# A pairwise-interaction tower: sums of two batches of products taken together on TensorE, with five product buffers and three weight buffers

## The chip, the cores and the metric

The kernel runs on one core of one Trainium2 chip. The metric is the device time of one execution in microseconds (us). The kernel before was run three times: 797.09, 798.48 and 800.0 us, median 798.48 us.

## The reference

For each of 2048 examples, 39 embedding rows `e` of 32 numbers are taken from 39 tables. Every pair of fields i < j gives one number through its own 32x32 matrix, and the 741 numbers, with 16 dense inputs, go through a small network:

```python
e = stack([tbl_f[ids[:, f]] for f in range(39)], axis=1)     # 2048 x 39 x 32
z = einsum('bpc,apc,bpa->bp', e[:, ROW], w, e[:, COL])         # 741 pairs
h = concatenate([z, dense_ctx], axis=1)
h = maximum(h @ W_top1 + b_top1, 0)                            # 757 -> 512
h = maximum(h @ W_top2 + b_top2, 0)                            # 512 -> 256
y = h @ W_top3                                                 # 256 -> 1
```

## The kernel before, in words

The examples are cut into NT = 4 tiles of 512 (variable `t`); examples lie along the free dimension. The 39 fields are grouped by four into 10 chunks of 128 partitions (4 fields x 32 numbers). The pairs of one tile are cut into NU = 200 units. A unit takes one field j against one chunk of up to four fields i, and so gives up to four of the 741 numbers. Units are worked in an order written out by hand (PHASES), two at a time in a step (UPS = 2) and four at a time in a batch (UPB = 4, SPB = 2 steps), so a tile has 50 batches (NBAT) and 100 steps (NS).

A unit goes through three stages.

1. `interact` (L538, matmul at L553): TensorE multiplies the unit's weights `w4` with the stacked field `e4` into PSUM `u_ps`. `u_ps` has room for two steps: step s waits until step s-2 has been multiplied (L541).
2. `multiply` (L844, instruction at L851): VectorE multiplies the two units of a step, straight from `u_ps`, with the embeddings `eT` into a product buffer `prod`. There are PR = 4 product buffers of one step each. Step s waits for its matmuls (L846) and until step s-PR has been summed (L848).
3. `reduce` (L564, matmul at L577): TensorE sums each product over 32 partitions with a 0/1 matrix `sel`, into one of the four 32-partition quadrants of PSUM `z_ps`. A batch has four such matmuls, each of them two matmul records in the trace. Units in different quadrants run at the same time; the quadrant of each unit is fixed by PLACES. Six `z_ps` tiles fill per tile of examples; ScalarE copies each to `zT` when its last unit is summed (`take_z`, L721 and L784 to L789).

The order on TensorE is written out (L639 to L656). For batch b: the two steps of `interact`; a piece of the top network of the tile before (`mlp_piece`, L590 to L594, two records each; none in the first tile, and 34 or 36 of the 50 batches have one otherwise); `reduce` of batch b-1; a `turn` (transposes of gathered rows into `t_ps`, L513), if one is due; and table look-ups (`look_up`, L532), if any are due. A look-up finds rows of the small tables by multiplying bf16 parts of the table with 0/1 matrices `one_hot`, which VectorE makes (L839) one batch ahead. Look-ups, too, write 32-partition quadrants. In the last tile, batches 40 to 49 also begin the top network for that tile itself (`early_piece`, L604), and `finish` (L606) completes it.

The order on VectorE (L881 to L893) for batch b: the two multiplies, then `split_chunk` if a chunk is complete, then the `one_hot` of batch b+1.

SyncE issues the loads in an order of its own (L479 to L493). Weights come as 25 pieces per tile (8 units, two batches each) into a ring `w4` of WR = 4 places. At every second batch the piece that stands WR-1 = 3 pieces ahead is loaded (`bring_piece`, L402), after the steps of batch b-1 have been issued (`s_u`, L410). On the same queue stand the stores of `parts` and the loads of `e4`. GpSimd gathers rows of the big tables, paced by the count of multiplies (L388).

Of the kernel before, what the change touches and what calls it, by code (L numbers as in the profile page):

```python
# [81 lines left out]
UPB = 4  # L82
NBAT = NU // UPB
# [28 lines left out]
ER = 4  # L112
PW = 8
NPW = NU // PW
WR = 4
ES = 4

PACED_FROM, PACE_LEAD = 96, 40

E4_SLOT = {0: 0, 1: 2, 2: 3, 3: 1, 7: 2, 8: 3, 4: 0, 5: 1, 6: 0, 9: 1}  # L120
OS = 3
PR = 4

TWO_PLACES = (0, 1, 2, 3, 7)

# [110 lines left out]
def mlp_pieces(batch, last):  # L236
    return [piece for piece, b in zip(MLP, MLP_AT[last]) if b == batch]


def ends_tile(tile):  # L240
    return max(u for u in range(NU) if PLACES[u][0] == tile)
# [10 lines left out]
def tower(nc, tables, ids, hot_ids, hot_rows, dense, w, w1, b1, w2, b2, w3, sel_in, ident_in, y):  # L252
# [4 lines left out]
    with ExitStack() as ctx:  # L257
        def sb(name, shape, dt=F32):
            return ctx.enter_context(nc.sbuf_tensor(name, shape, dt))

        def sem(name):
            return ctx.enter_context(nc.semaphore(name))

        w4 = sb("w4", [P, WR, PW * P], F32R)
        eT = sb("eT", [P, NG + len(TWO_PLACES), NB])
        e_rows = sb("e_rows", [P, ER, TPG, P])
        parts = sb("parts", [P, 2, 2, NB], F32R)
        e4 = sb("e4", [P, ES, C, NB], F32R)
        prod = sb("prod", [P, PR, UPS, NB])
        zT = sb("zT", [P, 2, NZ, NB])  # L270
# [72 lines left out]
        s_wout = [sem(f"s_wout{r}") for r in range(2)]  # L343
        s_w4 = [sem(f"s_w4{r}") for r in range(WR)]
        s_rows = [sem(f"s_rows{r}") for r in range(ER)]
# [19 lines left out]
        def e_slot(t, g):  # L365
            return NG + TWO_PLACES.index(g) if t % 2 and g in TWO_PLACES else g
# [34 lines left out]
        def _(sp):  # L401
            def bring_piece(t, p):  # L402
                n = NPW * t + p
                if n >= NPW * NT:
                    return
                if t == 0:
                    prep = [k for k, (a, b) in enumerate(PREP_UNITS) if a <= PW * p < b][0]
                    sp.wait_ge(s_wout[prep % 2], 64 * (prep // 2 + 1))
                if n >= WR:
                    sp.wait_ge(s_u, (n - WR + 1) * PW // UPS)  # L410
                sp.dma_start(w4[:, n % WR, :].bitcast(F32), w_rows.rearrange("a h x n -> (a h x) n")[:, PW * P * p:PW * P * (p + 1)]
                             ).then_inc(s_w4[n % WR], 16)

# [19 lines left out]
            def store_parts(c):  # L433
                t, g = c
                n = POS[c]
                rows = D * fields_in(g)
                here = scratch[t, g, 0:fields_in(g)].rearrange("j a h n -> (j a) h n")
                sp.wait_ge(s_eh, n + 1)
                sp.dma_start(here[:, 0, :], parts[0:rows, n % 2, 0, :].bitcast(F32)).then_inc(s_scr[n % 2], 16)
                sp.wait_ge(s_el, n + 1)  # L440
                sp.dma_start(here[:, 1, :], parts[0:rows, n % 2, 1, :].bitcast(F32)).then_inc(s_scr[n % 2], 16)
# [30 lines left out]
            stack_chunk((0, 0))  # L472
            stack_chunk((0, 1))
            store_parts((0, 2))
            bring_piece(0, 2)
            stack_chunk((0, 2))
            sp.dma_start(dense_g[:, :, :, :], dense.rearrange("t p n d -> p t (n d)").rearrange("p t (n d) -> p t n d", d=DENSE)).then_inc(s_dense, 16)

# [17 lines left out]
        def _(pe):  # L496
# [67 lines left out]
            def reduce(t, batch):  # L564
                pe.wait_ge(s_mul, NS * t + SPB * (batch + 1))
                if batch == NBAT - 1:
                    add_dense(t)
                for n in range(SPB * batch, SPB * (batch + 1)):
                    slots = [e_slot(t, UNITS[UPS * n + i][1]) for i in range(UPS)]
                    for i in range(UPS):  # L570
                        u = UPS * n + i
                        tile, quad, row = PLACES[u]
                        z = NZ * t + tile
                        if u in OPENS_TILE and z >= 2:
                            pe.wait_ge(s_zc, z - 1)
                        place = i if slots[0] <= slots[1] else 1 - i
                        last = nc.tensor.matmul(z_ps[D * quad:D * quad + D, z % 2, :],  # L577
                                                sel[:, D - 1 - row:2 * D - 1 - row], prod[:, (NS * t + n) % PR, place, :],
                                                start=u in OPENS, stop=u in CLOSES, skip_group_check=True)
                    last.then_inc(s_red, 1)  # L580
# [25 lines left out]
            def finish(t):  # L606
                pe.wait_ge(s_mul, NS * (t + 1))
                for m in (2, 3):
                    for k in range(NZ - 1):
                        if k == NZ - 2:  # L610
                            pe.wait_ge(s_zc, NZ * t + NZ - 1)
                        nc.tensor.matmul(end_ps[m], w1s[:, k, m * P:m * P + P], zT[:, t % 2, k, :], start=k == 0, stop=False)  # L612
                reduce(t, NBAT - 1)
                pe.wait_ge(s_zc, NZ * (t + 1))
                for m in range(H1 // P):
                    nc.tensor.matmul(end_ps[m], w1s[:, NZ - 1, m * P:m * P + P], zT[:, t % 2, NZ - 1, :],
                                     start=False, stop=True).then_inc(s_m, 1)
                for k in range(H1 // P):
                    pe.wait_ge(s_mc, NI * t + k + 1)
                    for m in range(H2 // P):  # L620
                        last = nc.tensor.matmul(end_ps[ITEM[2, m]], w2s[:, k, m * P:m * P + P], h1[:, k, :],  # L621
                                                start=k == 0, stop=k == H1 // P - 1)
                        if k == H1 // P - 1:
                            last.then_inc(s_m, 1)
                for k in range(H2 // P):
                    pe.wait_ge(s_mc, NI * t + ITEM[2, k] + 1)
                    last = nc.tensor.matmul(end_ps[ITEM[3, 0]][0:1, :], w3s[:, k:k + 1], h2[:, t % 2, k, :],
                                            start=k == 0, stop=k == H2 // P - 1)
                last.then_inc(s_m, 1)
# [9 lines left out]
            for t in range(NT):  # L639
                for b in range(NBAT):  # L640
                    for x in range(SPB):
                        interact(t, SPB * b + x)
                    if t:
                        for piece in mlp_pieces(b, t == NT - 1):
                            mlp_piece(t - 1, *piece)
                    if b:
                        reduce(t, b - 1)
                    elif t:
                        reduce(t - 1, NBAT - 1)
                    for c in TURNS.get(NBAT * t + b, ()):  # L650
                        turn(c)
                    for c, k in TAKES.get(NBAT * t + b, ()):
                        look_up(c, k)
                    if t == NT - 1:
                        for m, k in EARLY.get(b, ()):
                            early_piece(t, m, k)  # L656
            finish(NT - 1)

        @block.scalar
        def _(act):  # L660
# [109 lines left out]
            for t in range(NT):  # L770
                for b in range(NBAT):
                    if t == 0 and b in PREPS:
                        weights_high(PREPS[b])
                        weights_rest(PREPS[b])
                    if t == 0 and b in PREP_LOADS:
                        load_weights(PREP_LOADS[b])
                    if t == 0 and b == LAST_TABLE_BATCH:
                        table_high(HOT_CHUNKS[-1])
                        table_middle(HOT_CHUNKS[-1])
                    if t:  # L780
                        for layer, m, k in mlp_pieces(b, t == NT - 1):
                            if k == LAYER_INPUTS[layer] - 1:
                                take_mlp(t - 1, layer, m, m_ps[:, :])
                    for tile in range(NZ):  # L784
                        done = ends_tile(tile) // UPB + 1
                        if done == b:
                            take_z(t, tile)
                        elif t and done == NBAT and b == 0:
                            take_z(t - 1, tile)  # L789
                    for c in COMPLETE.get(NBAT * t + b, ()):  # L790
                        take_chunk(c)
            t = NT - 1
# [6 lines left out]
        def _(dve):  # L799
# [44 lines left out]
            def multiply(t, n):  # L844
                s = NS * t + n
                dve.wait_ge(s_u, s + 1)  # L846
                if s >= PR:
                    dve.wait_ge(s_red, s - PR + 1)  # L848
                a, b = sorted(e_slot(t, UNITS[UPS * n + i][1]) for i in range(UPS))
                e = eT[:, a:b + 1:b - a, :] if a != b else eT[:, a:a + 1, :].broadcast_to([P, UPS, NB])  # L850
                nc.vector.tensor_tensor(prod[:, s % PR, :, :], u_ps[:, s % 2, :, :], e, ALU.mult).then_inc(s_mul, 1)  # L851

# [100 lines left out]
```

## Time and profile before

| | us |
|---|---|
| median of three runs | 798.48 |
| the profiled execution | 801.8 |
| its span, first to last instruction | 799.6 |
| TensorE matmuls busy | 725.3 (91%) |
| VectorE busy | 635.5 (79%) |
| GpSimd busy | 422.2 (53%) |
| ScalarE busy | 94.2 (12%) |

Busy time is the time in which an engine has an instruction in work. The ends of matmuls are modelled and matmuls overlap, so the start of one group to the start of the next says more than a duration. The mean granted TensorE clock was 0.966 of full speed; the stretches with less lie in the first 170 us and for a moment near 239 us.

### The profile page before, as it was taken

The numbers are of one execution on the slowest core, as the hardware profiler recorded it, in microseconds if no ns is written. First come the engines' busy times: TensorE is split into PE (matmuls) and PEld (weight loads), VectorE is DVE, ScalarE is ACT, GpSimd is POOL, SyncE is SP. The second block draws the span as 40 slices with busy tenths as digits, with TensorE's granted clock in tenths as the row PEclk, the third lists the DMA queues.
The fourth block names the chain that finished last, engine by engine and source line by source line (L and its number), as shares of the span: only waits on it lengthen the run. The fifth ranks groups of instructions, "written<-read, shape, count | busy, mean of one in ns | idle before, by whom it ended". The sixth has DMA issues, their size and how long they took to land.

```text
span 799.6 us, 11291 instructions
## 1 busy us (share of the span) xinstructions
PE 725.3 (91%) x4378; PEld 289.6 (36%) x4378; DVE 635.5 (79%) x792; ACT 94.2 (12%) x170; POOL 422.2 (53%) x463
## 2 busy tenths in 40 slices
PE   1647387899989999999999999999999999999998
PEld 0212132333323344444333344444333444443343
DVE  3738679899987999889987898879969887778650
ACT  3211101011101000101111010110111010011002
POOL 6899999931565555555556555555655565100000
PEclk9777789999999999999999999999999999999999
DMA  7694838668878638264765655446765445443300
GB/s 212 227 321 168 280 96 276 224 198 302 287 254 300 246 90 261 66 220 160 249 207 169 220 133 197 134 146 227 232 221 158 157 153 195 163 137 94 118 0 1
DMA packets 75713, 149.88 MB, mean 187 GB/s; under 512 B 13621, under 2 KB 22920, under 8 KB 75532
## 3 DMA queue, kind: packets, MB, share of 16 engines
q1 hardware_dynamic: 52772, 125.30, 45.4%
q10 hardware_dynamic: 10600, 17.55, 6.4%
q0 software_dynamic: 12288, 6.32, 5.2%
q8 instruction: 35, 0.57, 0.3%
q14 instruction: 18, 0.15, 0.1%
HBM read 115.49 MB, written 33.62 MB: 186 GB/s over the span
## 4 chain that ended last, share of the span: by engine, by line
PE 73%; DVE 13%; DMA 6%; issue 5%; ACT 2%; ACTq 1%; SPq 0%; DVEq 0%
PE z_ps L577 23%; PE u_ps L553 22%; PE t_ps L532 10%; PE m_ps L590 8%; DVE prod L851 7%; DVE one_hot L839 4%; PE m_ps L592 3%; DMA e<-scratch 3%; PE t_ps L513 2%; DMA w_rows<-h 1%; PE u_ps L612 1%; ACTq L710 1%; PE u_ps L621 1%; DMA h<-in_w_dram 1%; PE m_ps L594 1%
## 5 line engine op out<-in xcount | busy, mean ns | idle before, releaser
L851 DVE TENSOR_TENSOR prod<-u_ps,eT 128x1024 f32<-128x1024 f32 x400 | 469.8, 1217 | 100.5 <-PE u_ps L553 100.1
L389 POOL DMA_INDIRECT e_rows<-in_tbl_dram,idx x384 | 379.1, 987 | 263.3 <-DVE prod L851 190.1
L553 PE MATMUL u_ps<-e,w 128*128 128x512 f32 x800 | 256.3, 434 | 45.0 <-DMA e<-scratch 21.6
L577 PE MATMUL z_ps<-prod,sel 128*32 128x512 f32 x1600 | 264.1, 614 | 0.0
L553 PEld LDWEIGHTS u_ps<-e,w 128*128 128x128 f32 x800 | 133.7, 190 | 184.8 <-DVE prod L851 86.7
L532 PE MATMUL t_ps<-one_hot,tb 125*32 125x512 bf16 x1560 | 158.6, 405 | 11.3 <-DVE one_hot L839 11.2
L839 DVE TENSOR_SCALAR one_hot<-hot_idx,row 125x512 bf16<-125x512 f16 (+2 forms) x320 | 136.3, 479 | 9.8 <-PE t_ps L532 7.7
L532 PEld LDWEIGHTS t_ps<-one_hot,tb 125*32 125x32 bf16 x1560 | 57.7, 101 | 109.5 <-issue 76.6
L577 PEld LDWEIGHTS z_ps<-prod,sel 128*32 128x32 f32 x1600 | 43.9, 108 | 139.4 <-issue 112.7
L590 PE MATMUL m_ps<-zT,w1s 128*128 128x512 f32 x144 | 73.5, 592 | 0.0
L671 ACT CAST parts<-t_ps 128x512 fp32r<-128x512 f32 (+1 forms) x40 | 23.5, 587 | 263.3 <-PE t_ps L532 158.7
L397 POOL MEMSET w1s<- 128x512 f32 x75 | 43.1, 574 | 0.0
L724 ACT COPY zT<-z_ps 128x512 f32<-128x512 f32 x24 | 14.1, 588 | 206.0 <-PE z_ps L577 206.0
L805 DVE TENSOR_TENSOR parts<-eT,parts 128x512 fp32r<-128x512 f32 (+1 forms) x40 | 27.2, 680 | 3.4 <-ACT eT L676 3.4
L590 PEld LDWEIGHTS m_ps<-zT,w1s 128*128 128x128 f32 x144 | 27.1, 188 | 6.3
L513 PE MATMUL t_ps<-ident,e_rows 128*128 128x128 f32 (+2 forms) x112 | 19.0, 294 | 6.4 <-ACT eT L676 6.4
L592 PE MATMUL m_ps<-h,w2s 128*128 128x512 f32 x48 | 24.5, 592 | 0.0
L676 ACT COPY eT<-t_ps 128x512 f32<-128x512 f32 (+1 forms) x40 | 23.6, 591 | 0.0
L513 PEld LDWEIGHTS t_ps<-ident,e_rows 128*128 128x128 f32 (+2 forms) x112 | 11.6, 136 | 29.9 <-issue 28.8
L731 ACT ACTIVATE h<-m_ps,b1s 128x512 f32<-128x512 f32 x13 | 9.0, 689 | 111.9 <-PE m_ps L590 110.7
L812 DVE TENSOR_TENSOR h<-h 128x512 fp32r<-128x512 f32 (+1 forms) x13 | 8.6, 662 | 10.7 <-ACT h L689 10.7
L689 ACT CAST h<-h 128x512 fp32r<-128x512 f32 (+1 forms) x13 | 7.9, 608 | 43.0 <-DMA w_rows<-h 30.1
(42 smaller groups left out, 101.1 us busy)
## 6 DMA issues: line engine op xcount, KB each, us to landing
w<-w_rows SPq DMA_DIRECT2D x100, 512.0 KB, 6.2
e<-scratch SPq DMA_DIRECT2D x72, 512.0 KB, 4.6
scratch<-parts SPq DMA_DIRECT2D x72, 256.0 KB
w_rows<-h ACTq DMA_DIRECT2D x48, 256.0 KB
e_rows<-in_tbl_dram,idx POOLq DMA_INDIRECT x384
hot_idx<-hot SPq DMA_DIRECT2D x12, 512.0 KB, 5.8
h<-in_w_dram ACTq DMA_DIRECT2D x12, 256.0 KB, 3.3
e<-scratch SPq DMA_DIRECT2D x8, 384.0 KB
```

Of the source, the lines that this page charges most:

```text
L389: pool.indirect_dma_start(e_rows[:, r, n, D * q:D * q + D], None, tables[f], bass.IndirectOffsetOnAxis(ap=idx[:, t, f * TPG + n:f * TPG + ...
L397: nc.gpsimd.memset(pause[:, :], 0.0).then_inc(s_pause, 1)
L513: last = nc.tensor.transpose(t_ps[0:hi, b * P:b * P + P], rows, ident[:, :])
L532: last = nc.tensor.matmul(t_ps[D * q:D * q + D, :], tb[0:HP, part, col:col + D], one_hot[0:HP, n % OS, here * NB:(here + 1) * NB], start=k ...
L553: last = nc.tensor.matmul(u_ps[:, s % 2, place, :], w4[:, p % WR, (u % PW) * P:(u % PW + 1) * P], e4[:, E4_SLOT[g], j - C * g, :], start=T ...
L577: last = nc.tensor.matmul(z_ps[D * quad:D * quad + D, z % 2, :], sel[:, D - 1 - row:2 * D - 1 - row], prod[:, (NS * t + n) % PR, place, :] ...
L590: last = nc.tensor.matmul(m_ps[:, :], w1s[:, k, m * P:m * P + P], zT[:, t % 2, k, :], start=k == 0, stop=stop)
L592: last = nc.tensor.matmul(m_ps[:, :], w2s[:, k, m * P:m * P + P], h1[:, k, :], start=k == 0, stop=stop)
L676: nc.scalar.copy(eT[0:rows, e_slot(t, g), :], t_ps[0:rows, :]).then_inc(s_et, 1)
L805: nc.vector.tensor_tensor(parts[0:rows, n % 2, 1, :], eT[0:rows, e_slot(t, g), :], parts[0:rows, n % 2, 0, :].bitcast(F32), ALU.subtract). ...
L839: last = nc.vector.tensor_scalar(one_hot[0:HP, n % OS, i * NB:(i + run) * NB], hot_idx[0:HP, LPOS[c] % 2, x * NB:(x + run) * NB], (row10 i ...
L851: nc.vector.tensor_tensor(prod[:, s % PR, :, :], u_ps[:, s % 2, :, :], e, ALU.mult).then_inc(s_mul, 1)
```

## The change

`SUMMED = 2` is new. `reduce` is now called in every second batch only: in an even batch b it is called for batch b-2 and then for batch b-1, at the place where it stood. In odd batches TensorE does no sums. At batch 0 of a tile the last two batches of the tile before are summed, and `finish` sums the last two. ScalarE's copies of `z_ps` move to the even batch in which the tile is complete. The product buffers are five in place of four, and the weight ring has three places in place of four; the weight piece loaded at an even batch is then two ahead, and the load of piece 2 before the loop falls away (it comes at batch 0).

```diff
-WR = 4
+WR = 3
...
-PR = 4
+PR = 5
+
+SUMMED = 2
...
             store_parts((0, 2))
-            bring_piece(0, 2)
             stack_chunk((0, 2))
...
-                reduce(t, NBAT - 1)
+                for back in range(SUMMED, 0, -1):
+                    reduce(t, NBAT - back)
...
-                    if b:
-                        reduce(t, b - 1)
-                    elif t:
-                        reduce(t - 1, NBAT - 1)
+                    if b % SUMMED == 0:
+                        for back in range(SUMMED, 0, -1):
+                            if b:
+                                reduce(t, b - back)
+                            elif t:
+                                reduce(t - 1, NBAT - back)
...
-                        done = ends_tile(tile) // UPB + 1
+                        done = SUMMED * (ends_tile(tile) // UPB // SUMMED + 1)
```

## Rows read from the trace of the kernel before

**Rows 1.** The page: busy time of the engines; the group of L553 with its idle time.
```profile
PE 725.3 (91%) x4378; PEld 289.6 (36%) x4378; DVE 635.5 (79%) x792; ACT 94.2 (12%) x170; POOL 422.2 (53%) x463
...
L553 PE MATMUL u_ps<-e,w 128*128 128x512 f32 x800 | 256.3, 434 | 45.0 <-DMA e<-scratch 21.6 <-DVE prod L851 20.9 <-issue 1.8
```

**Rows 2.** By stretch: us, busy of PE, PEld, DVE, ACT, POOL, PEclk, DMA share, GB/s.
```profile
642.98:734.30 91.32, 91.32 (x426) 37.30 (x423) 71.03 (x63) 10.78 (x18) 26.56 (x28) 1.00 0.47 155
769.80:799.60 29.80, 26.99 (x80) 10.48 (x78) 2.80 (x3) 5.28 (x8) 0.00 (x0) 1.00 0.00 1
121.00:260.70 139.70, 127.00 (x797) 47.09 (x797) 127.07 (x151) 17.30 (x32) 82.12 (x96) 0.96 0.79 266
```

**Rows 3.** The timeline, last tile, batch 33 (MLP, no look-up): start, us, instructions.
```profile
719.04 1.20 PE L553 MATMUL u_ps<-e,w 128*128 128x512 f32 x4
719.81 2.35 DVE L851 TENSOR_TENSOR prod<-u_ps,eT 128x1024 f32<-128x1024 f32 x2 [0.62 <-PE u_ps L553]
720.08 1.02 PE L592 MATMUL m_ps<-h,w2s 128*128 128x512 f32 x2
721.03 1.06 PE L577 MATMUL z_ps<-prod,sel 128*32 128x512 f32 x8
722.02 1.20 PE L553 MATMUL u_ps<-e,w 128*128 128x512 f32 x4
```

**Rows 4.** The timeline, last tile, batches 39 and 40 (no MLP before the sums).
```profile
737.21 1.19 PE L553 MATMUL u_ps<-e,w 128*128 128x512 f32 x4
737.97 4.62 DVE L851 TENSOR_TENSOR prod<-u_ps,eT 128x1024 f32<-128x1024 f32 x4
738.33 1.06 PE L577 MATMUL z_ps<-prod,sel 128*32 128x512 f32 x8
739.32 0.73 PE L553 MATMUL u_ps<-e,w 128*128 128x512 f32 x2
740.38 0.73 PE L553 MATMUL u_ps<-e,w 128*128 128x512 f32 x2 [0.33 <-DVE prod L851]
741.04 1.06 PE L577 MATMUL z_ps<-prod,sel 128*32 128x512 f32 x8
```

**Rows 5.** The timeline, last tile, batch 13: sums of a batch with a repeated quadrant.
```profile
657.28 1.90 PE L577 MATMUL z_ps<-prod,sel 128*32 128x512 f32 x8
659.11 0.50 PE L553 MATMUL u_ps<-e,w 128*128 128x512 f32 x1
```

**Rows 6.** The timeline, first tile, batches 9 to 11: no MLP, no look-up.
```profile
121.06 0.73 PE L553 MATMUL u_ps<-e,w 128*128 128x512 f32 x2 [0.88 <-DVE prod L851]
...
126.18 0.73 PE L553 MATMUL u_ps<-e,w 128*128 128x512 f32 x2
```

**Rows 7.** The timeline, second tile, batch 14: MLP and one look-up slice.
```profile
312.15 1.19 PE L553 MATMUL u_ps<-e,w 128*128 128x512 f32 x4
313.18 1.02 PE L590 MATMUL m_ps<-zT,w1s 128*128 128x512 f32 x2
314.13 1.07 PE L577 MATMUL z_ps<-prod,sel 128*32 128x512 f32 x8
315.01 0.83 PE L532 MATMUL t_ps<-one_hot,tb 125*32 125x512 bf16 x12
315.19 1.17 DVE L839 TENSOR_SCALAR one_hot<-hot_idx,row 125x512 bf16<-125x512 f16 x3
315.78 1.20 PE L553 MATMUL u_ps<-e,w 128*128 128x512 f32 x4
```

**Rows 8.** The timeline, second tile, VectorE between the multiplies of batches 6 and 7.
```profile
286.66 1.93 DVE L839 TENSOR_SCALAR one_hot<-hot_idx,row 125x512 bf16<-125x512 f16 x6
```

**Rows 9.** The view of tile w: weight loads, us from issue to landing.
```profile
DMA to landing us min/median/max: 3.4/6.2/9.1
```

**Rows 10.** The timeline, weight loads near the end of the first tile, and batch 48's start.
```profile
250.36 1.53 SPq L411 DMA_DIRECT2D w<-w_rows  x2
...
255.85 1.33 PE L553 MATMUL u_ps<-e,w 128*128 128x512 f32 x4
```

## The prediction

> **What bounds the kernel now.** I read the page's busy times first: TensorE 91%, VectorE 79% [rows 1]. The view by stretches shows where each is the limit [rows 2]: in the last tile's stretch without look-ups (batches 9 to 37) TensorE is busy for 91.32 of 91.32 us, VectorE for 71; in the first tile's main part both are busy for 127 of 139.7. Then I read the timeline batch by batch, since the change moves work between batches. A batch of the last tile [rows 3] is: matmuls of two steps at 719.04, an MLP piece at 720.08, sums at 721.03, next batch at 722.02, 2.98 us in all. VectorE starts its first multiply 0.77 us after the batch's start, needs 2.35 us for two, and is done 3.12 us after it. The next batch's second step must wait for that (two places in `u_ps`); it comes some 0.5 us after the next batch's start, at about 3.5, so the wait is hidden by 0.35 us. This cover is what the change touches.
>
> **When the cover is gone** is shown once, in batches 39 and 40 [rows 4]. Batch 39 has no MLP and lasts only 2.11 us (737.21 to 739.32). Its successor's second step starts at 740.38, held by VectorE: **3.17 us after the start of batch 39**, whatever TensorE had to do. After such a held step the sums follow 0.66 us later (741.04). I call 3.17 us the floor of a batch: from its first matmul to the next batch's second step.
>
> **The change, part by part.** Odd batches lose their sums, even ones have two.
>
> *What TensorE saves.* One round of sums (four units in four quadrants) takes 0.99 us up to the next unit matmul [rows 3], two rounds 1.83 [rows 5]. So two batches summed together cost 1.83 in place of 1.98, and the odd batch's switch from MLP matmuls to sums goes as well (0.95 against 0.86, two records of 0.43): about 0.25 us per pair. Before a look-up a round takes only 0.88 us [rows 7], twice that is 1.76, and 0.88 + 0.84 = 1.72 after: nothing to speak of is saved there, and the odd batch switches for its look-up anyhow. Where quadrants repeat, one batch takes two rounds and a pair three in place of 2+1, no difference; only in batches 42 and 43 (quadrants 1,2,3,1 and 2,3,1,2) do four rounds become three, -0.84 us, once per tile.
>
> *What the odd batch then costs.* Without sums and look-ups it is 1.04 + 0.86 = 1.90 us with an MLP piece and about 1 without; its successor's second step could come at 2.4, but the floor holds it until 3.17. VectorE is the limit there, though it is idle elsewhere. The pair (odd, even) is floor + 0.66 + MLP 0.86 + sums 1.83 = **6.52 us, before 5.96** (+0.56). Without MLP it is 3.17 + 0.66 + 1.83 = 5.66; before 5.12 in the first tile (121.06 to 126.18) [rows 6]: +0.54. The multiply of the even batch's second step now waits for a sum (five places: step s needs step s-5, summed in the same batch): sums' start + 1.07 + 1.21 for the multiply is 2.3 us after it, and the next batch's second step comes at 1.83 + 0.5 = 2.33. That wait just fits; it costs nothing as I sum it, and 0.1 us per pair if it misses.
>
> Odd batches with neither look-up nor turn, by the lists in the code: 11 in the first tile (9, 11, 19, 27, 37, 39 to 49), 7 in each of the next two (9, 39 to 49), 20 in the last (9 to 49 but 37): **45**. Less the 0.84 at batch 43 four times (-3.4), plus about 3 where the first tile's repeated quadrants were hidden behind VectorE and now lie behind the floor, less 1 to 2 where that tile waits for an `e4` load anyway (21.6 us of such idle time in all [rows 1]): 24.8 - 3.4 + 3 - 1.5 = **+23 us**.
>
> *Odd batches with look-ups.* With an MLP piece they last 1.03 + 0.95 + 0.76 = 2.74, second step after 3.3: above the floor, price 0 to 0.2 us since the `one_hot` (1.17 us) now follows a later multiply [rows 7]; 22 of these, +1 to +2. Without an MLP piece (some 7 per middle tile: 1, 7, 19, 21, 27, 33, 35, and the turn at 37) they last 1.9 to 2.6 and hit the floor: up to 0.7 each. The dearest is batch 7: 1.93 us of `one_hot` stand ahead of its multiplies [rows 8]; in batch 6 the second multiply now starts some 2.5 us into it, later by 0.8 or more, and all of this goes into batch 7: +1.2. I put 4 us on each middle tile, 2 on the last, 2 on the first: **+12** (bounds 4 and 18).
>
> *The end.* Batches 48 and 49 (three rounds) are summed after the last multiply, before only 49: **+0.8** in the stretch from 769.8 us [rows 2].
>
> *The buffers.* With three weight places a piece is issued one slot later (the time of the following piece). Landing takes 3.4 to 9.1 us [rows 9]. The later issue is still four batches ahead of use, some 12 to 14 us at 2.98 to 3.63 a batch [rows 3, 7]: free where SyncE's queue is on time. In the first tile it runs late in places, since stores and `e4` loads stand ahead on the queue: piece 24 would be issued when piece 25 was, at 250.36 us, its use is at batch 48, 255.85 [rows 10], and with the median 6.2 to 9.1 us to land it comes 1 to 3 us late. A late piece gives VectorE its time back in part, and the batches before are slower now. I take **+1**, bounds 0 and 6. The fifth product place costs nothing itself. Piece 2's load moves behind the `e4` loads of one chunk and the dense load on SyncE's queue, still four batches ahead of use; that frees these by one load. ScalarE's copies of `z_ps` come up to a batch later; only batch 44 of the last tile wants one at once (about 0.3 us, once).
>
> **Sum:** 23 + 12 + 0.8 + 1 = +36.8 us. The profiled execution took 801.8 us; the median of three is 798.5, 0.4% less, which changes the term by 0.1. On the median: **835 us**.
>
> The Trainium skill, TensorEngine Tiling, section "PSUM Bottleneck", says that tiling speeds TensorE up but not the reading of PSUM, which may then be the bottleneck. The rows agree in kind: what is saved on the tiled sums leaves VectorE's 2.35 us per batch from `u_ps` as they are. By the rule alone the saving would be nothing and the time 798; by the rows the order of the work makes it a loss.
>
> **The rivals.**
>
> *Faster: TensorE stays the bound.* Sums cost 0.11 us less when work of the same quadrant form follows (0.88 against 0.99), so each switch has a price, and half of them fall away. If VectorE's lateness were hidden, 45 pairs x 0.25 and 3.4 from batches 42/43 give -15: **784 us**. For it: TensorE 91% against VectorE 79%, and no idle TensorE in the last tile's stretch [rows 1, 2]. Against it: rows 4 show the very wait, in the same code, for a batch as short as the odd ones become. It would need the floor to be under 2.4 us. Chance 0.05. The Trainium skill, TensorEngine Tiling, section "Key Properties", has the rule behind this rival: changing the tiling mode drains TensorE. The rows have a switch at about 0.1 us, so the rule holds but is small.
>
> *Slower by half:* the odd batches with look-ups absorb their share (MLP and `one_hot` reorder themselves around the wait), and only the 45 count, without the 3 us of the first tile: +20, **818 us**. Chance 0.15; this is a matter of degree.
>
> *Slower by more:* the weight ring runs dry in the first tile (+6), the look-up batches take their full +18, and the miss of 0.1 per even batch comes (+4.5): 835 + 5 + 6 + 4.5 = **851 us**. Or TensorE's clock, 1.00 where it is never idle but 0.96 in the stretch with 9% idle [rows 2], falls with the new gaps; 4% of the 539 us after 260.7 is +21, 856. Chance 0.08.
>
> *No effect:* within 0.3% (about what a measurement of this kernel can tell from no change) only if savings and waits cancel. Chance 0.03.
>
> **How the numbers follow.** The forecast has 0.69. The range takes in the half case and two thirds of the way to the heavier one: 816 to 846. Faster 0.05, same 0.03, slower 0.92.
>
> **What the changed profile would show.** Right: in the last tile, batches 9 to 36, pairs of 6.5 us in place of 5.96; the second step of `u_ps` in each even batch separate from the first, with idle time released by the multiply, 3.17 us after the odd batch's start; sixteen sum records in 1.8 us; TensorE's idle time before L553 on VectorE up from 20.9 us [rows 1] to over 30, its busy share under 89%. The stretch from batch 9 to 37 of the last tile, 91.3 us before, takes 99. Wrong: if that stretch takes under 90, the floor doesn't hold and the first rival is true; if weight loads release TensorE for more than a few us, the ring is the cause; if clock falls under 0.95 after 260 us, the clock is.

## The result, and the profile after

The changed kernel takes **848.06 us** (median of 4 runs, 846.37 to 851.38) against 799.24 for the kernel before in the same session: ratio 1.0626, 95% interval [1.0578, 1.0673]. I had forecast 835 with a range of 816 to 846. The sign and most of the size are as forecast, but the result lies above the range.

The page of the changed kernel, its busy times, answers to [rows 1]:

```profile
span 846.7 us, 11291 instructions
...
PE 727.5 (86%) x4378; PEld 287.6 (34%) x4378; DVE 637.4 (75%) x792; ACT 94.1 (11%) x170; POOL 426.7 (50%) x463
```

The work is the same (TensorE 727.5 us busy, VectorE 637.4), the span is 47.1 us longer. TensorE now stands idle for 86.5 us ahead of its unit matmuls, 45.0 before. From the groups by shape, and then from the view of waits, what it waited for:

```profile
L855 DVE TENSOR_TENSOR prod<-u_ps,eT 128x1024 f32<-128x1024 f32 x400 | 475.4, 1217 | 148.3 <-PE z_ps L578 73.7 <-PE u_ps L554 73.7
L554 PE MATMUL u_ps<-e,w 128*128 128x512 f32 x800 | 269.0, 442 | 86.5 <-DVE prod L855 50.7 <-DMA e<-scratch 19.5 <-DMA w<-w_rows 13.7
```

```profile
PE u_ps L554 <- DVE prod L855: 50.7, 90, 6.2
...
PE u_ps L554 <- DMA w<-w_rows: 13.7, 6, 5.6
```

Two waits grew: for VectorE from 20.9 us to 50.7, and for weight loads from nothing to 13.7, which is the prediction's own sign that the ring is a cause. By stretches (the last tile's batches 9 to 37, the end from batch 49, and the first tile from batch 9), to be read against [rows 2]:

```profile
678.19:774.53 96.34, 90.87 (x407) 35.68 (x404) 67.84 (x60) 10.77 (x18) 25.97 (x28) 1.00 0.45 147
816.01:846.70 30.69, 26.77 (x80) 10.66 (x78) 2.35 (x2) 5.28 (x8) 0.00 (x0) 1.00 0.00 1
120.84:276.81 155.97, 123.37 (x788) 47.71 (x788) 127.47 (x151) 17.19 (x32) 83.00 (x96) 0.95 0.72 240
```

The first of these ends at the start of batch 37. The same batches took 87.98 us before (642.98 to 730.96 in the timeline), so they lose 8.4 us in 14 pairs. TensorE, never idle there before, now idles for 5.5. Up to the start of batch 38, where the prediction's window ends, it is 98.95 us after 91.31; I had said 99.

The timeline of one pair, batches 32 (even) and 33 of the last tile, answers to [rows 3, 4]:

```profile
756.92 0.72 PE L554 MATMUL u_ps<-e,w 128*128 128x512 f32 x2
758.05 0.73 PE L554 MATMUL u_ps<-e,w 128*128 128x512 f32 x2 [0.41 <-DVE prod L855]
758.62 1.02 PE L593 MATMUL m_ps<-h,w2s 128*128 128x512 f32 x2
759.58 1.92 PE L578 MATMUL z_ps<-prod,sel 128*32 128x512 f32 x16
760.75 1.23 DVE L855 TENSOR_TENSOR prod<-u_ps,eT 128x1024 f32<-128x1024 f32 x1 [1.62 <-PE z_ps L578]
761.43 1.32 PE L554 MATMUL u_ps<-e,w 128*128 128x512 f32 x4
762.20 2.35 DVE L855 TENSOR_TENSOR prod<-u_ps,eT 128x1024 f32<-128x1024 f32 x2 [0.23 <-PE u_ps L554]
762.59 1.02 PE L593 MATMUL m_ps<-h,w2s 128*128 128x512 f32 x2
763.48 0.73 PE L554 MATMUL u_ps<-e,w 128*128 128x512 f32 x2
```

The floor shows here. The even batch begins at 756.92, but its second step comes only at 758.05, released by VectorE. Sixteen sum records take 1.85 us (759.58 to 761.43), where two rounds apart take 1.98. The odd batch lasts 2.05 us, and the next even batch begins at 763.48; the pair is 6.56 us, before 5.96. VectorE idles for 1.62 us while it waits for the first sums, but that costs nothing in this pair: the multiply behind the wait ends at 761.98, and the odd batch's first matmuls are ready only at 762.20 (VectorE waits 0.23 us for them). From there its two multiplies take 2.35 us, and the odd batch is over before they are.

Where the 47.1 us are, from the starts of batch 1 of each tile in the two timelines (differences taken before rounding):

| stretch | before | after | difference |
|---|---|---|---|
| up to batch 1 of the first tile | 61.2 | 59.3 | -1.9 |
| first tile | 203.4 | 222.4 | +19.0 |
| second tile | 174.4 | 182.6 | +8.2 |
| third tile | 174.5 | 182.5 | +8.1 |
| last tile, batches 1 to 48 | 156.2 | 169.1 | +12.8 |
| batch 49 and the end | 29.8 | 30.7 | +0.9 |

### The profile page after: what moved, and what is told of

Its sections match the earlier page's. It is cut to its first block, busy times and chain, and to the rows that moved or that the text cites. A ratio compares the mean times of both kernels' runs of the same rounds, so it can differ in the third digit from the quotient of the medians.

```text
span 846.7 us, 11291 instructions
## 1 busy us (share of the span) xinstructions
PE 727.5 (86%) x4378; PEld 287.6 (34%) x4378; DVE 637.4 (75%) x792; ACT 94.1 (11%) x170; POOL 426.7 (50%) x463
## 4 chain that ended last, share of the span: by engine, by line
PE 57%; DVE 21%; issue 10%; DMA 8%; ACT 2%; ACTq 1%; SPq 1%; DVEq 0%
PE z_ps L578 21%; PE u_ps L554 16%; DVE prod L855 13%; PE t_ps L533 7%; PE m_ps L591 6%; DVE one_hot L843 5%; DMA w<-w_rows 4%; DMA scratch<-parts 2%; PE t_ps L514 1%; DMA e<-scratch 1%; PE m_ps L593 1%; PE u_ps L613 1%; ACTq L714 1%; DVE parts L809 1%; PE u_ps L623 1%
## 5 line engine op out<-in xcount | busy, mean ns | idle before, releaser
L855 DVE TENSOR_TENSOR prod<-u_ps,eT 128x1024 f32<-128x1024 f32 x400 | 475.4, 1217 | 148.3 <-PE z_ps L578 73.7
L391 POOL DMA_INDIRECT e_rows<-in_tbl_dram,idx x384 | 383.1, 998 | 297.6 <-DVE prod L855 235.7
L554 PE MATMUL u_ps<-e,w 128*128 128x512 f32 x800 | 269.0, 442 | 86.5 <-DVE prod L855 50.7
L578 PE MATMUL z_ps<-prod,sel 128*32 128x512 f32 x1600 | 236.1, 612 | 0.0
L554 PEld LDWEIGHTS u_ps<-e,w 128*128 128x128 f32 x800 | 128.8, 191 | 240.0 <-DVE prod L855 160.5
L533 PE MATMUL t_ps<-one_hot,tb 125*32 125x512 bf16 x1560 | 149.9, 402 | 12.1 <-DVE one_hot L843 11.6
L578 PEld LDWEIGHTS z_ps<-prod,sel 128*32 128x32 f32 x1600 | 52.0, 110 | 140.4 <-issue 121.6
L533 PEld LDWEIGHTS t_ps<-one_hot,tb 125*32 125x32 bf16 x1560 | 50.0, 100 | 105.4 <-issue 63.8
```

The source lines that it names most:

```text
L391: pool.indirect_dma_start(e_rows[:, r, n, D * q:D * q + D], None, tables[f], bass.IndirectOffsetOnAxis(ap=idx[:, t, f * TPG + n:f * TPG + ...
L533: last = nc.tensor.matmul(t_ps[D * q:D * q + D, :], tb[0:HP, part, col:col + D], one_hot[0:HP, n % OS, here * NB:(here + 1) * NB], start=k ...
L554: last = nc.tensor.matmul(u_ps[:, s % 2, place, :], w4[:, p % WR, (u % PW) * P:(u % PW + 1) * P], e4[:, E4_SLOT[g], j - C * g, :], start=T ...
```

## The experiments

Two theories stood after the result. **Theory:** the 3.17 us floor makes the loss of the later tiles (and part of the first), and the three-place weight ring the excess in the first. **Rivals:** the ring is the main cause; or the sums taken together are slow themselves. Twelve kernels were run. Every run is compared with the kernel before on the same chip, 797.5 us for the first four, 801.06 for the next four, 798.93 for the last.

### The weight ring

Run `ring3_alone` is the kernel before with

```diff
-WR = 4
+WR = 3
...
-            bring_piece(0, 2)
```

> The kernel before with the weight ring of three places and nothing else of the change (piece 2 is loaded in the loop). Theory (floor of 3.17 us per short batch for most of the loss, late weight pieces in the first tile for 10 us or so of it): +3 to +10 us over before, all of it in the first tile, with TensorE waiting for weight loads; the later tiles unchanged to 0.5 us each. Rival A (the ring is the main cause): +30 us or more. Rival B (the ring does nothing by itself): within 2 us.

Measured: 812.13 us, ratio 1.0173 [1.0113, 1.0234], so +14 us, more than I expected. The first tile takes 217.3 us in place of 203.4 (+13.9), the next two 174.5 and 174.4, as before. The last takes 157.3 in place of 156.2, all of it in batch 15, with no weight wait; it wasn't looked at further. TensorE waited for five weight loads, 12.1 us in all. Three of the late pieces in the timeline of `ring3_alone`:

```profile
235.89 1.16 PE L552 MATMUL u_ps<-e,w 128*128 128x512 f32 x4 [1.06 <-DMA w<-w_rows]
245.49 1.55 PE L552 MATMUL u_ps<-e,w 128*128 128x512 f32 x4 [3.89 <-DMA w<-w_rows]
267.12 2.04 PE L552 MATMUL u_ps<-e,w 128*128 128x512 f32 x4 [3.81 <-DMA w<-w_rows]
```

They are pieces 20, 21 and 24. On SyncE's queue these are the issues that bring the last two, with what stands ahead:

```profile
238.13 1.24 SPq L452 DMA_DIRECT2D e<-scratch  x2
239.47 1.49 SPq L411 DMA_DIRECT2D w<-w_rows  x3
250.49 0.32 SPq L439 DMA_DIRECT2D scratch<-parts  x1
253.26 0.32 SPq L441 DMA_DIRECT2D scratch<-parts  x1
...
256.38 1.31 SPq L452 DMA_DIRECT2D e<-scratch  x2
257.79 4.88 SPq L411 DMA_DIRECT2D w<-w_rows  x3
```

At 239.47 and at 257.79 several weight pieces leave together: the queue stood at a store or a stacked load, and the first piece behind it was due long before (piece 21 at batch 38, whose matmuls start at 229.10). Ahead of the second bunch stand also the loads of the top network's weights, which come once, at batch 44 of the first tile. With three places the first of each bunch is the one that TensorE wants next. So the ring is a cause by itself, nearly all of it in the first tile, but not the main one: 14 us of 47.

Two runs took the ring's loss out of the changed kernel. `pairs_ring4` is the changed kernel with

```diff
-WR = 3
+WR = 4
...
-ER = 4
+ER = 2
...
+            bring_piece(0, 2)
             stack_chunk((0, 2))
```

> The changed kernel with four weight places again; the room comes from two places for gathered rows in place of four. Theory: the weight waits of TensorE (13.7 us in the changed kernel's profile) go to about 0, time 848 less 8 to 13 us, plus what two gather places cost (next run); tiles two to four keep their +8, +8 and +13 us. Rival A (the ring is the main cause): back to within 10 us of before.

and `before_er2` is its control, the kernel before with `ER = 2` alone.

> Control for the run above: the kernel before with two places for gathered rows. Gathers run 40 multiplies ahead, two chunks or so, so I expect +0 to +5 us, in the first tile. Whatever it is, it is taken off the run above.

Measured: 842.31 us, ratio 1.0559 [1.0497, 1.0621], and 805.41 us, ratio 1.011 [1.0046, 1.0174]. No weight wait is left in `pairs_ring4`; the two gather places cost 8 us in the control, more than I expected, with 10.8 us of TensorE's waits for gathered rows. The changed kernel with a ring of four is 37 us behind the control. That difference is what the pairing of sums costs without the ring, the fifth product place included. The first tile takes 215.5 us against 207.7 in the control (+7.8, of the +19.0), and the later tiles keep their +8, +8 and +13.

`pairs_weights_first` moves one statement:

```diff
                 for b in range(NBAT):
...
+                    if b * UPB % PW == 0:
+                        p = b * UPB // PW + WR - 1
+                        bring_piece(t + p // NPW, p % NPW)
                     for c in COMPLETE.get(NBAT * t + b - 1, ()):
                         store_parts(c)
                     for c in STACKS.get(NBAT * t + b, ()):
                         stack_chunk(c)
-                    if b * UPB % PW == 0:
-                        p = b * UPB // PW + WR - 1
-                        bring_piece(t + p // NPW, p % NPW)
```

> The changed kernel with one move on SyncE's queue: in each batch the weight piece is issued ahead of the stores and stacked loads of that batch, ring of three kept. Theory (pieces are late because they stand behind those on the queue): weight waits of 13.7 us fall to under 5, time 838 to 843. If pieces are late because they land slowly (up to 10 us among the other loads), only 2 us or less are gained.

Measured: 838.66 us, ratio 1.0512 [1.045, 1.0574]; weight waits 2.3 us in place of 13.7, the first tile 213.3 in place of 222.4. So most of the lateness came from what stood ahead of the pieces on the queue. A fourth place takes the waits away too (`pairs_ring4`): a piece then has a slot more to wait on the queue. The one wait left here is for piece 24, which is issued at 251.13 and lets TensorE go on at 260.85, 9.7 us later, so a slow landing has a share as well.

### The floor

If VectorE's time from `u_ps` makes the loss, halving that time must remove it. Both kernels were run with multiplies of half the columns. The other half of each product is set to zero once before the loop (not shown in the cut), so half of each sum's examples are left out:

```diff
-                nc.vector.tensor_tensor(prod[:, s % PR, :, :], u_ps[:, s % 2, :, :], e, ALU.mult)
+                H = NB // 2
...
+                nc.vector.tensor_tensor(prod[:, s % PR, :, 0:H], u_ps[:, s % 2, :, 0:H], e, ALU.mult)
```

> The kernel before with multiplies of half the columns (the other half of each product stays zero, so half of the pair sums are left out). VectorE's pair takes some 1.2 us in place of 2.35; TensorE is the bound in tiles two to four, so they keep their time, and the first gains 5 to 20 us: 780 to 795.

> The changed kernel with the same half multiplies. The floor falls to 0.77 + 0.6 + 0.65 + 0.05 = 2.1 us, below the 2.4 that a short odd batch takes by itself. Theory: pairs of the last tile's stretch fall from 6.55 to 5.72 or so (TensorE's saving of 0.25 shows), tiles two to four are faster than in the half multiply of before by 2 to 6 us each, and the whole is within -15 to +5 us of it, the weight waits of the first tile being what is left. Rival (the loss isn't VectorE's time): the changed kernel stays 25 us or more behind.

Measured: 782.6 us for the kernel before, ratio 0.977 [0.9712, 0.9827], and 798.43 us for the changed one, ratio 0.9957 [0.9928, 0.9985]. On the whole the changed kernel is 16 us behind, outside what I expected; but the place matters. In tiles two and three it takes 170.5 and 171.4 us against 172.8 and 172.8, in the last 151.3 against 155.6: **faster in all three**, if by less than the 2 us I had expected in the third. The whole loss is in the first tile, 215.9 against 189.8, with 23.6 us of waits for weight loads (the faster a tile runs, the sooner it wants its pieces). The timeline of `pairs_half_mul`, batches 21 and 22 of the last tile:

```profile
685.31 1.19 PE L555 MATMUL u_ps<-e,w 128*128 128x512 f32 x4
686.07 1.29 DVE L858 TENSOR_TENSOR prod<-u_ps,eT 128x512 f32<-128x512 f32 x2 [1.17 <-PE u_ps L555]
686.34 1.02 PE L592 MATMUL m_ps<-zT,w1s 128*128 128x512 f32 x2
686.82 1.47 PE L555 MATMUL u_ps<-e,w 128*128 128x512 f32 x4
...
688.12 1.02 PE L592 MATMUL m_ps<-zT,w1s 128*128 128x512 f32 x2
689.07 1.92 PE L579 MATMUL z_ps<-prod,sel 128*32 128x512 f32 x16
...
690.93 0.50 PE L555 MATMUL u_ps<-e,w 128*128 128x512 f32 x1
```

The pair is 5.62 us (685.31 to 690.93), against 6.56 in the changed kernel and 5.96 before. Sixteen sum records still take 1.86 us. The saving that the first rival of the prediction named is there, 0.3 us a pair, once VectorE's time doesn't stand over it. The run also settles another rival, that VectorE's wait for the sums makes the loss: that wait grew from 73.7 us in the changed kernel to 129.9 here, and the pair is shorter than before.

The same floor can be filled with work. `pairs_mlp_odd` gives the odd batches two MLP pieces and the even ones none, with the same 34 pieces:

```diff
-MLP_AT = {last: spread_mlp(last) for last in (False, True)}
+ODD = {True: list(range(5, 39, 2)), False: [5, 9, 11, 13, 15, 17, 19, 23, 25, 29, 31, 37, 39, 41, 43, 45, 47]}
+MLP_AT = {last: [b for b in ODD[last] for x in range(2)] for last in (False, True)}
```

> The changed kernel with the same 34 MLP pieces per tile, two in each of 17 odd batches in place of one in most batches. Theory of the floor: an odd batch with two pieces lasts 1.04 + 1.71 = 2.75 us, its successor's second step comes at 3.3, past the floor of 3.17; an even batch without one is 1.12 + 1.83 = 2.95. A pair of the last tile's stretch is 5.7 us, against 6.55 changed and 5.96 before. 17 pairs in the last tile x 0.85, some 8 in each middle tile x 0.6 to 0.85: 25 to 27 us off, 820 to 825. Rival (the loss lies in the wait of the multiply for the sums, 73.7 us of VectorE's idle time, or in the doubled sums themselves): those stay, and the time moves by under 5 us.

`before_mlp_odd` has the same edit on the kernel before.

> Control: the kernel before with the same placing of the MLP pieces. Its batches are then 1.12 + 1.0 = 2.1 us and 3.8 us; the short ones hit the floor (3.17 to the next second step, then 0.66 less the 0.57), so a pair costs 3.17 + 1.8 + 1.41 or so, 6.3 to 6.5 in place of 5.96: +5 to +15 us. If placing alone were good, it would be faster than before.

Measured: 830.63 us, ratio 1.0363 [1.0312, 1.0413], for the changed kernel, 17 us less than the 848.06 without the edit; 814.3 us, ratio 1.0181 [1.0126, 1.0235], for the one before, which loses 13 to 15. So the placing helps only where the odd batches are short: with one round of sums in each batch it makes the batches without a piece short in their turn. The pair in `pairs_mlp_odd`, batches 33 and 34 of the last tile:

```profile
744.40 1.33 PE L555 MATMUL u_ps<-e,w 128*128 128x512 f32 x4
745.17 2.36 DVE L856 TENSOR_TENSOR prod<-u_ps,eT 128x1024 f32<-128x1024 f32 x2 [0.23 <-PE u_ps L555]
745.57 1.88 PE L594 MATMUL m_ps<-h,w2s 128*128 128x512 f32 x4
746.88 1.49 PE L555 MATMUL u_ps<-e,w 128*128 128x512 f32 x4
...
748.30 1.92 PE L579 MATMUL z_ps<-prod,sel 128*32 128x512 f32 x16
749.47 1.23 DVE L856 TENSOR_TENSOR prod<-u_ps,eT 128x1024 f32<-128x1024 f32 x1 [0.30 <-PE z_ps L579]
750.16 0.50 PE L555 MATMUL u_ps<-e,w 128*128 128x512 f32 x1
```

5.76 us (744.40 to 750.16), where I had said 5.7, and below the 5.96 of before. The last tile's batches 9 to 36 take 86.7 us against 96.3 changed, 88.0 before and 93.9 in the control. VectorE's wait for the sums falls as well here (33.6 us), so this run alone would not tell the floor from that wait; `pairs_half_mul` does. The whole falls short of my 820 to 825: the two middle tiles gain 4.5 and 5.5 us, about what I had, but the last gains 8.1 where I had 14.5. Its batches 37 to 48 take 43.3 us, 41.5 without the edit, and TensorE's granted clock is at half for 3.4 us of them, from 766.2. The first tile gains 0.5 us, with 19.5 us of waits for weight loads.

### Repeated quadrants

Rows 5 gave another price: a batch whose units share a quadrant takes 0.84 us more. Twelve batches of each tile do (0, 1, 4, 12, 16, 23, 24, 40, 42, 43, 44, 49), in whichever kernel. The four-row slots of each `z_ps` tile can be dealt to other quadrants freely. A search over such swaps left four (0, 11, 45, 48); the edit replaces `PLACES = place_sums()` by that list. `before_quadrants` is the kernel before with it:

```diff
-PLACES = place_sums()
+PLACES = [(0, 1, 16), (0, 1, 17), (0, 0, 24), (0, 0, 16), (0, 0, 4), (0, 1, 19), (0, 2, 12), (0, 3, 4),
...
```

> The kernel before with the units of each z_ps tile dealt to other quadrants, so that 4 batches per tile of examples have a repeated quadrant in place of 12. Same arithmetic, same order. A repeated quadrant costs 0.84 us where TensorE is the bound: 8 x 0.84 = 6.7 us off each of tiles two to four, 0 to 4 off the first: 774 to 780. Rival: the sums' second rounds run beside look-ups and VectorE's work, and under 10 us in all comes off.

Measured: **777.24 us, ratio 0.9725 [0.97, 0.9751]**, 22 us less than before and the fastest kernel of the study. Tiles two and three take 167.7 and 167.8 us (-6.7 each, as worked out), the last 149.6 (-6.6), the first 200.6 (-2.8). The rival is out: the second rounds were on the path.

`before_quadrants_first` adds the weight pieces first on SyncE's queue.

> The run above with weight pieces issued ahead of stores and stacked loads. The ring of four has no weight waits before, so nothing should come of it: within 3 us of the run above; stores delayed by a wait for the unit matmuls could cost up to 5.

Measured: 781.6 us, ratio 0.977 [0.9746, 0.9795]: 4 us slower. With four places no weight load was late to begin with. The profiles are 4.3 us apart, 1.9 of it ahead of batch 1 of the first tile, 1.0 in the first tile and 1.5 in the second; TensorE's waits for `e4` loads are 25.7 us against 24.3. That the move delays stores and stacked loads, which now stand behind it, is likely but not shown.

`pairs_quadrants` is the changed kernel with the quadrants.

> The changed kernel with the same quadrants. Its even batches are past the floor and shrink with each round saved, but the pair with four rounds turned into three before is lost as a gain: 7 rounds x 0.84 = 5.9 us off each of the last three tiles, and 0 to 5 off the first (weight waits take back what is won there): 825 to 830, the loss against its own kernel before still 45 to 55 us.

Measured: 829.57 us, ratio 1.0381 [1.0342, 1.042]; 176.9, 176.8 and 163.3 us in tiles two to four, 5.7 to 5.8 less each. Against `before_quadrants` it is 52 us behind, as before the cure.

`pairs_all` has all three: quadrants, MLP pieces in odd batches, weight pieces first.

> The changed kernel with all three cures: quadrants as above, two MLP pieces in each odd batch, weight pieces first on SyncE's queue. Gains should add: 848 - 9 - 17 - 20 = 800 to 806. If they add, pairs of sums can be brought to the time of before but not below it with the same cures (before_quadrants).

Measured: 799.31 us, ratio 1.0001 [0.9976, 1.0026]. The cures add up, to 49 us where I had 42 to 48, and bring the pairing of sums to the time of before, not under it; one of the three alone brings the kernel before to 777.

## Why the prediction was right or wrong

The prediction's sum by its own terms, against the profile's +47.1:

| term | forecast | measured |
|---|---|---|
| 34 odd batches without look-up or turn, tiles two to four | +16.2 | +16.5 |
| odd batches with look-ups, tiles two to four | +10 | +12.6 |
| the end | +0.8 | +0.9 |
| first tile, without the ring | +8.7 | +6.8 |
| weight ring | +1 | +10 |

The first term's forecast is 34 x 0.55 less three times 0.84, and the first tile's is 11 x 0.55 - 0.84 + 3 - 1.5 + 2. The measured ones of tiles two to four are sums over pairs of the two timelines. The first tile's is `pairs_ring4` against `before_er2` with the stretch ahead of it (+7.8 - 1.0), and the ring's what is left of the first tile's 19.0 - 1.9. The ring alone cost 13.9 there; in the changed kernel it costs less, probably since its batches are slower and give each piece more time.

**Right: the floor.** The pair was 6.56 us where I had 6.52; the second step of the even batch comes 3.18 us after the odd batch's start, where I had 3.17; sixteen sum records take 1.85, where I had 1.83. `pairs_half_mul` shows that this is VectorE's time. The pair of batches 43 and 44, where the sums of 42 and 43 are taken together, gains (7.82 to 7.38 in the second tile), since four rounds become three. The last tile's pairs cost 0.59 to 0.61 each in the main, just above the forecast's 0.56. The seven of the second tile lie between -0.43 and +0.90 us and come to 2.9, where I had 3.0: that this sum fits so well is partly luck.

**Right, somewhat small: the look-up batches.** Those with an MLP piece cost nothing, on average (-0.05 to +0.2 us, but 0.76 for batches 29 and 30). Batch 7 costs 1.03 where I had 1.2; batches 1 and 2 cost 0.8, 33 and 34 0.8, 37 and 38 0.9, 21 and 22 0.6, the others without a piece 0.1 to 0.2. I put 4 us on a middle tile, and it is 5.2. The timeline of the changed kernel in the second tile, batch 7, answers to [rows 8]:

```profile
303.82 1.23 DVE L855 TENSOR_TENSOR prod<-u_ps,eT 128x1024 f32<-128x1024 f32 x1 [1.56 <-PE z_ps L578]
304.96 1.93 DVE L843 TENSOR_SCALAR one_hot<-hot_idx,row 125x512 bf16<-125x512 f16 x6
305.15 1.21 PE L554 MATMUL u_ps<-e,w 128*128 128x512 f32 x4
...
306.81 2.34 DVE L855 TENSOR_TENSOR prod<-u_ps,eT 128x1024 f32<-128x1024 f32 x2
308.07 0.50 PE L554 MATMUL u_ps<-e,w 128*128 128x512 f32 x1 [0.30 <-DVE prod L855]
```

The `one_hot` instructions run until 306.9, so the batch's multiplies begin at 306.81, 1.66 us into it; before they began 1.27 us in. The multiply ahead of the `one_hot` had waited 1.56 us for the sums, so here that wait is on the path. No run changed the number of product places alone, so what more of them would give back in such batches is open.

**Wrong: the weight ring.** The step that failed is "I take +1, bounds 0 and 6". The mechanism was named, but I worked out one piece (24, 1 to 3 us late; it held TensorE for 4.5), assumed that late pieces overlap with VectorE's lateness, and left out the others. The changed kernel's timeline:

```profile
184.76 1.17 PE L554 MATMUL u_ps<-e,w 128*128 128x512 f32 x4 [2.38 <-DMA w<-w_rows]
...
243.98 1.62 PE L554 MATMUL u_ps<-e,w 128*128 128x512 f32 x3 [5.57 <-DMA w<-w_rows]
...
268.54 2.04 PE L554 MATMUL u_ps<-e,w 128*128 128x512 f32 x4 [4.52 <-DMA w<-w_rows]
270.51 3.64 PE L578 MATMUL z_ps<-prod,sel 128*32 128x512 f32 x16
274.08 0.94 PE L514 MATMUL t_ps<-ident,e_rows 128*128 128x128 f32 x4
```

The waits are for pieces 13, 21 and 24. For piece 21 the prediction's own rule gives it from the timeline of the kernel before: pieces 22, 23 and 24 are issued together at 235.30, and piece 21 is wanted at batch 42, 236.22.

```profile
235.30 1.49 SPq L411 DMA_DIRECT2D w<-w_rows  x3
236.22 0.98 PE L553 MATMUL u_ps<-e,w 128*128 128x512 f32 x3
```

Issued one slot later, at 235.30, and with the median 6.2 us to land, piece 21 comes 5.3 us late. The same rule makes piece 20 late by 1.2 us and piece 24 by 0.7, 7 us in all; with 9.1 us to land, pieces 13 and 17 are late too, and all five together make some 20. So the timeline that I had already put the term at 7 or more, past my upper bound of 6. In the changed kernel piece 21 is issued at 237.73, and TensorE can go on at 243.98. With that term at 10 the forecast would have been 844, inside the range. Of the 4 us beyond that, the other terms make 1.3 (the look-up batches were 2.6 too small, the first tile 1.9 too large); for the rest, the medians lie further apart (848.06 and my 798.48: 49.6 us) than the two profiles (47.1).

**The rivals.** The faster one is denied as a whole (TensorE would have to be the bound in odd batches), but its price, 0.25 us a pair, shows at 0.3 once VectorE is out of the way. The heavier one, with the ring at +6 and the look-up batches at +18, was nearest in its result, with the shares the other way round. Of the prediction's second heavy case, TensorE's clock, there is nothing after the first tile: the granted clock is 1.00 from 274.7 us on. In the first tile it has a small part. The stretch from batch 9 has 0.95 against 0.96, and two of its low stretches lie at the two longest weight waits: the granted clock is 0.50 of full speed (1.2 in place of 2.4 GHz) from 240.6 to 247.4 and from 267.9 to 274.7, where TensorE had stood idle for 5.57 and 4.52 us. The lines above show the price: four unit matmuls take 1.97 us and sixteen sum records 3.57 (270.51 to 274.08), against 1.04 [rows 3] and 1.85. In the two batches after the waits that is some 4 us, by my estimate from such differences, and it stands inside the +10 of the ring; the kernel before has low stretches of its own there (10.2 us in all, the changed one 17.1).

## What to carry to other kernels

When work is bunched in every second round of a loop, cost the round that is left short, not the one that is full: with two buffers between the engines, its successor's second step can't start before the other engine has worked off the whole round. That floor may be found in the trace of before, in a round that is short for another reason. A ring's depth is judged by each entry's slack between landing and use, for every entry and above all where the issuing queue stands still, and not by the mean or by one entry.

## What the runs showed that I had not expected

Dealing the sums to other quadrants, which changes no instruction's count, took 22 us off (0.9725). The same move of weight loads up the queue gained 9 us with three places and cost 4 with four. Around each of the two longest waits for weights TensorE's granted clock fell to half for 6.8 us, so that such a wait cost more than its own length. And with half the columns multiplied, the weight waits of the first tile rose from 13.7 to 23.6 us: a faster tile is also one that wants its weights earlier.
